# Moving VectorE's state update ahead of the output steps, and the scaled residual one slot earlier

## The chip, the cores and the metric

The kernel runs on one core of a Trainium2 chip. The metric is the device time of one launch in microseconds; less is better. The profile's engine names are PE (TensorE matmuls), PEld (TensorE weight loads), DVE (VectorE), ACT (ScalarE), POOL (GpSimd) and SP (the queue that issues the DMAs).

## The reference

The input is eight sequences of 512 tokens with 128 features. Each goes through a layer norm, a state-space attention block with its own RMS norm and residual, a second layer norm and a mixture of expert feed-forward networks with a residual. What touches this change is the scan of the attention block:

```python
def step(h, inp):
    x_c, dt_c, B_c, C_c = inp
    lcs = jnp.cumsum(dt_c * A, axis=1)
    lcsT = jnp.transpose(lcs, (0, 2, 1))
    M = jnp.exp(jnp.where(mask, lcsT[:, :, :, None] - lcsT[:, :, None, :], -jnp.inf))
    G = jnp.einsum('blhn,bihn->bhli', C_c, B_c)
    intra = jnp.einsum('bhli,bihp->blhp', M * G, x_c)
    inter = jnp.einsum('blh,blhn,bhpn->blhp', jnp.exp(lcs), C_c, h)
    total_decay = jnp.exp(lcsT[:, :, -1])
    h_new = total_decay[:, :, None, None] * h + jnp.einsum('bhl,blhp,blhn->bhpn', M[:, :, -1, :], x_c, B_c)
    return (h_new, intra + inter)
...
y = y + x_h * D[None, None, :, None]
y = y * jax.nn.silu(z)
y = rmsnorm(y, w_norm_out)
return residual + y @ w_out_proj
```

The output of a chunk (`intra + inter`) and its new state (`h_new`) both need products of the chunk, but not each other.

## The kernel before

A sequence is worked in chunks of 128 tokens, four of them (`c` = 0 to 3), for 8 heads as 4 pairs. The work of three sequences is interleaved: `body(s, prev, older)` runs 24 slots `i` (0 to 23), in which every engine does the attention of sequence `s` and the feed-forward blocks of sequence `prev` (and the last four blocks of `older`). Each engine runs a list of instructions in the order in which the code writes them; semaphores join the lists.

**Feed-forward blocks.** In slot `i` block `b = i - 4` is begun. TensorE makes three products of it into a bank of PSUM (`first`, L360 to L362, out of `fTh`/`fTl`), ScalarE writes `act_h` (L757), VectorE writes `act_l` (`act_low`, L1105), and two slots later TensorE makes three more (`second`, L562 to L564). There are two such banks, so `first(b)` waits only for the `act_l` of block `b - 2`. Every fourth block VectorE also writes a product of the expert's output and its weights (`routed_out`, L1113), before `second` may overwrite its bank, and GpSimd adds it up (L1299).

**The scan.** From slot 12 on a chunk takes three slots.

- Step 0: TensorE makes the segments of the decays (`segments`, L441) in two halves of four matmuls. The first half writes bank `MAIN[0]` and waits until VectorE has read the outputs of the last chunk there (`y_steps`). The second half writes `MAIN[1]` and waits for `state_step`, the state update of the last chunk, which reads `MAIN[1]`. Then come `b_tokens` (L451). ScalarE turns the segments into `decay` (eight instructions, L781), then copies `btok` (L785). GpSimd makes `xw` (L1286) and masks `decay` (L1290).
- Step 1: TensorE transposes the last chunk's `yz` (`y_transposes`, L498), after `btok` has been copied, since both use one bank. Then come the Gram products (L464). VectorE multiplies them by the decay into `mg` (L984).
- Step 2: TensorE makes, in this order, the products with the state (L473), the chunk's own part of the new state (L478, `s_psum`), and the products within the chunk (L485, `y_psum`). VectorE's `attend(..., 2)` follows: it waits for `y_psum`, makes `yt` (L991 for c = 0; L995, L999, L1001 after that) and `yz` (L1006); then, for c below 3, `state_m = state * tdx` (L1010) and the two halves of `state` (L1023, for c = 0 a copy, L1021). Only after these does it turn to the slot's `act_low`.

At the end of the chunk's slot TensorE is at `first` and `second`, and then at `segments` of the next chunk.

**The residual.** `residual(s)` makes two small columns (L913, L914) and four products of 128x128 (`xr`, L917). It reads only what `norm1` left; `add_residual` reads `xr` in the next body, and the DMA of the next sequence's `x_in` waits for it. VectorE's order in slots 8 to 11 is: `dt_decay` (L946 to L950), `act_low` of slots 8 and 9, `l_parts` (L955 to L963, it waits for ScalarE's `ecs_ready`), `residual`, `gT_copy` (L1100), `act_low` of slot 10, `lT_copy` (L971). TensorE waits for `l_parts` at L426 and for `gT_copy` at L537.

In sequence 0 there are no feed-forward blocks yet; in its place stands the folding of the weights (L580, L583, DVE L889, ACT L699, POOL L1226 and L1231).

Of the kernel before, what the change touches and what calls it, by code (L numbers as in the profile page):

```python
# [7 lines left out]
ALU = mybir.AluOpType  # L8
# [6 lines left out]
P = 128  # L15
NCH = 4
# [4 lines left out]
NP = NH // 2  # L21
HD = DI // NH
# [18 lines left out]
def nth(s, per, k):  # L41


    if isinstance(s, int) and s * per + k <= 0:
        return None
    return s * per + k


def is_seq(s, n):

    return isinstance(s, int) and s == n


def build(nc, a, out):
# [4 lines left out]
    with ExitStack() as ctx:  # L59
        def sb(name, shape, dt=F32):  # L60
            return ctx.enter_context(nc.sbuf_tensor(name, shape, dt))

        def sem(name):
            return ctx.enter_context(nc.semaphore(name))
# [5 lines left out]
        MAIN = bank[4:8]  # L70
# [83 lines left out]
        tdx = sb("tdx", [P, NCH, NP])  # L154
# [9 lines left out]
        state = sb("state", [P, NP, 2 * HD])  # L164
        state_m = sb("state_m", [P, NP, 2 * HD])
# [86 lines left out]
        y_psum = sem("y_psum")  # L252
        s_psum = sem("s_psum")
        state_step = sem("state_step")
# [613 lines left out]
        def _(dve):  # L868
            v_ = nc.vector
# [42 lines left out]
            def residual(s):  # L912
                v_.tensor_scalar(one_rs[:], rs1[:, 0, :], 1.0, None, ALU.add).then_inc(xr_scales, 1)  # L913
                v_.tensor_tensor(mean_rs[:], mv1[:, :, 0], rs1[:, 0, :], ALU.mult).then_inc(xr_scales, 1)  # L914
                dve.wait_ge(xr_scales, nth(s, 2, 2))
                for c in range(NCH):
                    v_.tensor_scalar(xr[:, c, :], x_in[:, c, :], one_rs[:, c:c + 1], mean_rs[:, c:c + 1], ALU.mult, ALU.subtract)\  # L917
                        .then_inc(xr_ready, 1)
# [17 lines left out]
            def dt_add(s, c):  # L936
                dve.wait_ge(sz_ready, nth(s, 4, c + 1))
                v_.tensor_tensor(dtv[:, c, :], MAIN[(c + 2) % 4][:, DI:2 * DI], b_dt[:], ALU.add).then_inc(dtv_ready, 1)

            def dt_clamp(s):  # L940
                dve.wait_ge(dtv_ready, nth(s, 4, 4))
                v_.tensor_scalar(sp[:], dtv[:], CLAMP, None, ALU.min).then_inc(dt_clamped, 1)

            def dt_decay(s):
                dve.wait_ge(dt_log, nth(s, 1, 1))
                v_.tensor_tensor(dtv[:], dtv[:], sp[:], ALU.max).then_inc(dt_steps, 1)  # L946
                dve.wait_ge(dt_steps, nth(s, 3, 1))
                v_.tensor_reduce(dsum[:], dtv[:].rearrange("p c (h d) -> p (c h) d", d=HD), AX_X, ALU.add).then_inc(dt_steps, 1)
                dve.wait_ge(dt_steps, nth(s, 3, 2))
                v_.tensor_tensor(dta[:].rearrange("p (c h) -> p c h", h=NH), dsum[:].rearrange("p (c h) -> p c h", h=NH),  # L950
                                 a_neg[:].unsqueeze(1).to_broadcast([P, NCH, NH]), ALU.mult).then_inc(dt_steps, 1)
# [13 lines left out]
            def l_parts(s):  # L965
                dve.wait_ge(ecs_ready, nth(s, 4, 4))
                three_parts(TR[:, 0:32].rearrange("p (c h) -> p c h", h=NH), lparts, rem1, rem2, lpart_steps, s, 5, 0)

            def lT_copy(s):
                dve.wait_ge(lT_psum, nth(s, 1, 1))  # L970
                v_.tensor_copy(lT[:], TR_BF[0:3 * NH, :]).then_inc(lT_ready, 1)  # L971

            def c_copy(s, b):
                dve.wait_ge(proj_psum, nth(s, 14, b + 11))
                v_.tensor_copy(CT[:, b, :], MAIN[b][:]).then_inc(c_ready, 1)

            def attend(s, c, step):
                if step == 1:
                    for hf in range(2):
                        dve.wait_ge(g_psum, nth(s, 8, 2 * c + hf + 1))  # L980
                        dve.wait_ge(decay_masked, nth(s, 8, 2 * c + hf + 1))
                        if hf == 0 and (v := nth(s, 4, c)) is not None:
                            dve.wait_ge(y_psum, v)
                        v_.tensor_tensor(mg[:, hf, :, :].rearrange("p n l -> p (n l)"), MAIN[2 + hf][:],  # L984
                                         decay[:, hf, :, :].rearrange("p n l -> p (n l)"), ALU.mult).then_inc(mg_ready, 1)
                if step == 2:

                    dve.wait_ge(y_psum, nth(s, 4, c + 1))
                    dve.wait_ge(xd_ready, nth(s, 4, c + 1))
                    if c == 0:  # L990
                        v_.tensor_tensor(yt[:], MAIN[0][:, 0:DI], xd[:], ALU.add).then_inc(y_steps, 1)  # L991
                        dve.wait_ge(y_steps, nth(s, 10, 1))
                    else:
                        first = 3 * c - 2
                        v_.tensor_tensor(yt[:].rearrange("p (h d) -> p h d", h=NH),  # L995
                                         MAIN[0][:, DI:2 * DI].rearrange("p (h d) -> p h d", h=NH),
                                         ecs[:, c, :].unsqueeze(2).to_broadcast([P, NH, HD]), ALU.mult).then_inc(y_steps, 1)
                        dve.wait_ge(y_steps, nth(s, 10, first + 1))
                        v_.tensor_tensor(yt[:], MAIN[0][:, 0:DI], yt[:], ALU.add).then_inc(y_steps, 1)  # L999
                        dve.wait_ge(y_steps, nth(s, 10, first + 2))  # L1000
                        v_.tensor_tensor(yt[:], yt[:], xd[:], ALU.add).then_inc(y_steps, 1)  # L1001
                        dve.wait_ge(y_steps, nth(s, 10, first + 3))
                    if (v := nth(s, 4, c)) is not None:
                        dve.wait_ge(ssq_ready, v)
                        dve.wait_ge(yT_psum, v)
                    v_.tensor_tensor(yz[:], yt[:], sz[:, c, :], ALU.mult).then_inc(yz_ready, 1)  # L1006
                    if c < NCH - 1:
                        first = (0, 2, 5)[c]
                        if c > 0:
                            v_.tensor_tensor(state_m[:], state[:], tdx[:, c, :].unsqueeze(2).to_broadcast([P, NP, 2 * HD]),  # L1010
                                             ALU.mult).then_inc(state_step, 1)
                            dve.wait_ge(state_step, nth(s, 8, first + 1))
                            first += 1
                        dve.wait_ge(s_psum, nth(s, 3, c + 1))
                        if (v := nth(s, 4, c + 1 if c > 0 else 0)) is not None:
                            dve.wait_ge(y_psum, v)
                        own = MAIN[1][:, 0:256].rearrange("p (n d) -> p n d", n=NP)
                        for t in range(2):
                            q, d = slice(64 * t, 64 * t + 64), slice(HD * t, HD * t + HD)
                            if c == 0:  # L1020
                                v_.tensor_copy(state[q, :, d], own[q, :, d]).then_inc(state_step, 1)  # L1021
                            else:
                                v_.tensor_tensor(state[q, :, d], own[q, :, d], state_m[q, :, d], ALU.add).then_inc(state_step, 1)  # L1023
                        dve.wait_ge(state_step, nth(s, 8, first + 2))

            def mean_square(s):
                dve.wait_ge(ssq_ready, nth(s, 4, 4))
# [97 lines left out]
            def scan_part(s, i):  # L1125
                last = is_seq(s, n_seq - 1)
                if i == 2:
                    dt_add(s, 0)
                    dt_add(s, 1)
                if i == 3:  # L1130
                    dt_add(s, 2)
                if i == 4:
                    dt_add(s, 3)
                    dt_clamp(s)
                if i == 7:
                    c_copy(s, 0)
                if i == 8:
                    dt_decay(s)
                if i == 10:
                    l_parts(s)  # L1140
                    residual(s)
                if i == 11:
                    lT_copy(s)
                if i >= CHUNKS_FROM:
                    attend(s, *divmod(i - CHUNKS_FROM, 3))
                if i == 15 and not last:
                    norm1(s + 1)
                if i == 18 and not last:
                    norm1_apply(s + 1)

            def body(s, prev, older):
                for i in range(NBLK):
# [5 lines left out]
                    if s is not None:  # L1158
                        if i == 0:
                            conv(s, 0, (0, 1))  # L1160
                        scan_part(s, i)
# [185 lines left out]
```

## Time and profile before

| | |
|---|---|
| median of 3 runs | 759.35 us (758.93 to 760.9) |
| the profiled execution | 760.49 us, its span 758.4 us |
| mean granted TensorE clock | 0.946 |
| PE busy | 656.0 us (86%) |
| PEld busy | 514.7 us (68%) |
| DVE busy | 477.1 us (63%) |
| ACT busy | 359.9 us (47%) |
| POOL busy | 176.7 us (23%) |

A time of an engine is the sum over its instructions; the rest of the span it waited. The profiled execution took 2.1 us more than its span, and 1.14 us more than the median. The granted clock is the share of full speed (2.4 GHz) that TensorE had; 0.5 is 1.2 GHz.

### The profile page before, as it was taken

How to read it: one execution, taken by the hardware profiler on the slowest of the kernel's cores; microseconds unless marked ns; L12 is line 12 of the kernel's file. 1: busy time of each engine (PE TensorE's matmuls, PEld its weight loads, DVE VectorE, ACT ScalarE, POOL GpSimd, SP SyncE). 2: the span in 40 equal slices, each digit the busy share in tenths (PEclk: the TensorE clock that was granted, in tenths of full speed). 3: DMA queues.
4: the chain of work that ended last, by engine and by line, in shares of the span. 5: the costliest groups of instructions: out<-in, count | busy, mean ns of one | idle time of the engine just before them, and what ended most of it. 6: DMA issues, size and time to landing. Idle time of an engine off the chain costs nothing.

```text
span 758.4 us, 11829 instructions
## 1 busy us (share of the span) xinstructions
PE 656.0 (86%) x3890; PEld 514.7 (68%) x3890; DVE 477.1 (63%) x1148; ACT 359.9 (47%) x837; POOL 176.7 (23%) x249
## 2 busy tenths in 40 slices
PE   4477869989889988989889988999989988988896
PEld 3355857677767766777767766777767766776664
DVE  6654266566766587467767587467767587465544
ACT  3624136634564346644655346544655346542252
POOL 7146110323013210323014110323014110232002
PEclk9879579999999999999999999999999999999799
DMA  7000000000000000000000000000000000000000
GB/s 230 8 15 2 1 0 1 15 1 1 0 29 1 1 1 1 29 1 1 0 28 0 0 0 8 20 0 0 0 28 0 0 1 15 1 1 0 15 1 14
DMA packets 12345, 8.89 MB, mean 12 GB/s; under 512 B 1259, under 2 KB 10902, under 8 KB 12310
## 3 DMA queue, kind: packets, MB, share of 16 engines
q1 hardware_dynamic: 12310, 8.44, 3.6%
q8 instruction: 20, 0.33, 0.2%
q14 instruction: 15, 0.12, 0.1%
HBM read 6.34 MB, written 2.10 MB: 11 GB/s over the span
## 4 chain that ended last, share of the span: by engine, by line
PE 49%; DVE 24%; issue 6%; ACT 5%; POOL 0%; DVEq 0%; POOLq 0%; ACTq 0%
PE bank L485 7%; PE bank L360 6%; PE bank L362 5%; PE bank L361 5%; PE bank L464 4%; PE bank L562 4%; PE bank L563 3%; PE bank L564 3%; DVE act_l L1105 3%; PE bank L478 2%; PE bank L473 2%; ACT decay L781 2%; DVE cv L933 2%; PE bank L506 1%; PE bank L441 1%
## 5 line engine op out<-in xcount | busy, mean ns | idle before, releaser
L757 ACT ACTIVATE act_h<-bank 128x512 fp32r<-128x512 f32 x192 | 116.8, 609 | 205.2 <-PE bank L362 203.2
L1105 DVE SCALAR_TENSOR_TENSOR act_l<-bank,act_h 128x512 fp32r<-128x512 f32 x192 | 131.2, 687 | 117.3 <-ACT act_h L757 115.3
L360 PE MATMUL bank<-fTl,w1h 128*128 128x512 f32 x192 | 92.2, 480 | 22.1 <-DVE fTl L1060 11.2
L1299 POOL TENSOR_TENSOR late<-late 128x512 f32<-128x512 f32 x32 | 41.4, 1293 | 259.7 <-DVE late L1113 259.7
L781 ACT ACTIVATE decay<-bank,lneg 128x128 f32<-128x128 f32 x256 | 71.2, 382 | 35.4 <-PE bank L441 35.4
L562 PE MATMUL bank<-act_l,w2h 128*128 128x512 f32 x192 | 80.1, 417 | 3.7 <-DVE act_l L1105 2.2
L563 PE MATMUL bank<-act_h,w2l 128*128 128x512 f32 x192 | 78.0, 406 | 0.0
L362 PE MATMUL bank<-fTh,w1h 128*128 128x512 f32 x192 | 77.9, 406 | 0.0
L564 PE MATMUL bank<-act_h,w2h 128*128 128x512 f32 x192 | 77.6, 404 | 0.0
L361 PE MATMUL bank<-fTh,w1l 128*128 128x512 f32 x192 | 77.3, 402 | 0.0
L360 PEld LDWEIGHTS bank<-fTl,w1h 128*128 128x128 f32 x192 | 36.8, 191 | 44.5 <-DVE act_l L1105 32.6
L485 PE MATMUL bank<-xs,mg 128*128 128x32 f32 x512 | 65.2, 283 | 0.0
L485 PEld LDWEIGHTS bank<-xs,mg 128*128 128x128 f32 x512 | 63.0, 201 | 0.7
L1286 POOL TENSOR_TENSOR xw<-xs,decay 128x128 f32<-128x128 f32 x48 | 19.5, 406 | 181.6 <-ACT decay L781 116.8
L995 DVE TENSOR_TENSOR yt<-bank,ecs 128x256 f32<-128x256 f32 x24 | 10.2, 425 | 68.5 <-PE bank L485 68.5
L984 DVE TENSOR_TENSOR mg<-bank,decay 128x512 f32<-128x512 f32 x64 | 41.1, 682 | 16.7 <-PE bank L464 16.4
L562 PEld LDWEIGHTS bank<-act_l,w2h 128*128 128x128 f32 x192 | 36.9, 192 | 18.4 <-DVE act_l L1105 6.2
L564 PEld LDWEIGHTS bank<-act_h,w2h 128*128 128x128 f32 x192 | 37.2, 194 | 9.1
L362 PEld LDWEIGHTS bank<-fTh,w1h 128*128 128x128 f32 x192 | 37.1, 193 | 8.9
L563 PEld LDWEIGHTS bank<-act_h,w2l 128*128 128x128 f32 x192 | 37.3, 194 | 7.7
L1290 POOL TENSOR_SCALAR_AFFINE_SELECT decay<-decay 128x508 f32<-128x508 f32 x64 | 41.2, 644 | 0.0
L464 PE MATMUL bank<-CT,BT 64*128 64x128 f32 x512 | 40.0, 299 | 0.0
(193 smaller groups left out, 1258.3 us busy)
## 6 DMA issues: line engine op xcount, KB each, us to landing
x_in<-L_attn_hidden_dram SPq DMA_DIRECT2D x8, 256.0 KB, 2.8
out_dram<-late SPq DMA_DIRECT2D x8, 256.0 KB, 2.8
late<-L_ffn_sw_dram SPq DMA_DIRECT2D x2, 512.0 KB, 6.3
late<-L_ffn_rw_dram SPq DMA_DIRECT2D x1, 1024.0 KB, 6.7
CT<-L_attn_w_in_proj_dram SPq DMA_DIRECT2D x1, 772.0 KB, 4.6
b_dt<-L_attn_b_dt_dram SPq DMA_DIRECT2D x1, 128.0 KB, 3.3
w_out_raw<-L_attn_w_out_proj_dram SPq DMA_DIRECT2D x1, 128.0 KB, 3.5
rows<-L_ffn_sb_dram SPq DMA_DIRECT2D x1, 4.0 KB
```

The source lines that it names most:

```text
L360: mm(dst, stat_h, mov_l, start=True, stop=False)
L361: mm(dst, stat_l, mov_h, start=False, stop=False)
L362: return mm(dst, stat_h, mov_h, start=False, stop=True)
L464: ins = mm(MAIN[2 + hf][:, at(n)], BT[q, n, at(c)], CT[q, n, at(c)], start=True, stop=True)
L485: ins = mm(MAIN[0][:, h * HD:(h + 1) * HD], mg[:, hf, n, :], xs[:, c, h * HD:(h + 1) * HD], start=True, stop=True)
L562: mm(FOUT[:], w2h[:, g, k, :], act_l[:, r, :], start=begins, stop=False)
L563: mm(FOUT[:], w2l[:, g, k, :], act_h[:, r, :], start=False, stop=False)
L564: mm(FOUT[:], w2h[:, g, k, :], act_h[:, r, :], start=False, stop=ends).then_inc(second_done, 1)
L757: nc.scalar.activation(act_h[:, b % RING, :], HID[b % 2][:], ACT.Relu).then_inc(act_h_ready, 1)
L781: ins = nc.scalar.activation(decay[:, hf, n, :], MAIN[hf][:, at(n)], ACT.Exp, bias=lneg[:, c, 2 * n + hf:2 * n + hf + 1])
L1105: v_.scalar_tensor_tensor(act_l[:, r, :], HID[b % 2][:], 0.0, f(act_h[:, r, :]), ALU.max, ALU.subtract)\
L1299: g.tensor_tensor(acc, acc, term, ALU.add).then_inc(acc_ready, 1)
```

## The change

In step 2 the whole state update (L1010, L1021 and L1023) moves ahead of the wait for `y_psum`, so it waits for `s_psum` alone, and its own wait for `y_psum` goes. `residual(s)` is called in slot 9, ahead of that slot's `act_low`, and no longer in slot 10 behind `l_parts`. No instruction is added or removed on any engine.

```diff
                 if step == 2:
 
+                    if c < NCH - 1:
+                        first = (0, 2, 5)[c]
+                        if c > 0:
+                            v_.tensor_tensor(state_m[:], state[:], tdx[:, c, :].unsqueeze(2).to_broadcast([P, NP, 2 * HD]),
+                                             ALU.mult).then_inc(state_step, 1)
+                            dve.wait_ge(state_step, nth(s, 8, first + 1))
+                            first += 1
+                        dve.wait_ge(s_psum, nth(s, 3, c + 1))
+                        own = MAIN[1][:, 0:256].rearrange("p (n d) -> p n d", n=NP)
+                        for t in range(2):
+                            q, d = slice(64 * t, 64 * t + 64), slice(HD * t, HD * t + HD)
+                            if c == 0:
+                                v_.tensor_copy(state[q, :, d], own[q, :, d]).then_inc(state_step, 1)
+                            else:
+                                v_.tensor_tensor(state[q, :, d], own[q, :, d], state_m[q, :, d], ALU.add).then_inc(state_step, 1)
+                        dve.wait_ge(state_step, nth(s, 8, first + 2))
+
                     dve.wait_ge(y_psum, nth(s, 4, c + 1))
                     dve.wait_ge(xd_ready, nth(s, 4, c + 1))
...
                     v_.tensor_tensor(yz[:], yt[:], sz[:, c, :], ALU.mult).then_inc(yz_ready, 1)
-                    if c < NCH - 1:
-                        first = (0, 2, 5)[c]
...
-                        dve.wait_ge(s_psum, nth(s, 3, c + 1))
-                        if (v := nth(s, 4, c + 1 if c > 0 else 0)) is not None:
-                            dve.wait_ge(y_psum, v)
...
-                        dve.wait_ge(state_step, nth(s, 8, first + 2))
...
                 if i == 8:
                     dt_decay(s)
+                if i == 9:
+                    residual(s)
                 if i == 10:
                     l_parts(s)
-                    residual(s)
```

## Rows read from the trace of the kernel before

**Rows 1.** Waits, whole span: us in total, times, longest us.

```profile
DVE yt L995 <- PE bank L485: 68.5, 24, 5.7
...
PE bank L441 <- DVE state L1023: 15.3, 14, 1.3
...
PE bank L537 <- DVE gT L1100: 7.8, 7, 1.1
```

**Rows 2.** VectorE's groups by line: count, busy us, mean ns, idle before.

```profile
L1023 DVE TENSOR_TENSOR state<-bank,state_m 64x128 f32<-64x128 f32 x32 | 9.2, 289 | 1.7 <-DVE state_m L1010 0.8
...
L917 DVE TENSOR_SCALAR xr<-x_in,one_rs,mean_rs 128x128 f32<-128x128 f32 x32 | 8.9, 342 | 0.3
...
L1010 DVE TENSOR_TENSOR state_m<-state,tdx 128x256 f32<-128x256 f32 x16 | 6.7, 418 | 0.0
...
L1021 DVE COPY state<-bank 64x128 f32<-64x128 f32 x16 | 4.6, 285 | 0.2
```

**Rows 3.** Timeline, sequence 3, chunk 1 to 2: start, duration, instruction, idle before.

```profile
321.05 0.69 DVE L1105 SCALAR_TENSOR_TENSOR act_l<-bank,act_h 128x512 fp32r<-128x512 f32 x1 [0.25 <-ACT act_h L757]
...
321.77 1.06 PE L478 MATMUL bank<-xw,btok 128*128 128x64 f32 x8
...
324.62 0.43 DVE L995 TENSOR_TENSOR yt<-bank,ecs 128x256 f32<-128x256 f32 x1 [2.88 <-PE bank L485]
...
326.00 0.39 PE L441 MATMUL bank<-lT,pick_head 24*128 24x128 bf16 x4
...
326.79 0.61 DVE L1023 TENSOR_TENSOR state<-bank,state_m 64x128 f32<-64x128 f32 x2
327.46 0.39 PE L441 MATMUL bank<-lT,pick_head 24*128 24x128 bf16 x4 [1.07 <-DVE state L1023]
...
328.95 1.32 POOL L1299 TENSOR_TENSOR late<-late 128x512 f32<-128x512 f32 x1 [8.23 <-DVE late L1113]
...
329.74 0.38 PE L498 MATMUL bank<-ident,yz 128*128 128x128 f32 x2
```

**Rows 4.** Timeline, sequence 3, chunk 0 to 1.

```profile
314.74 0.62 PE L441 MATMUL bank<-lT,pick_head 24*128 24x128 bf16 x8
...
317.96 0.44 PE L498 MATMUL bank<-ident,yz 128*128 128x128 f32 x2 [0.61 <-ACT btok L785]
```

**Rows 5.** Timeline, sequence 3, chunk 2 to 3.

```profile
337.72 0.39 PE L441 MATMUL bank<-lT,pick_head 24*128 24x128 bf16 x4
...
343.37 0.39 PE L562 MATMUL bank<-act_l,w2h 128*128 128x512 f32 x1
```

**Rows 6.** Timeline, sequence 5, chunk 2 to 3.

```profile
508.76 0.93 PE L441 MATMUL bank<-lT,pick_head 24*128 24x128 bf16 x8
...
513.58 0.19 PEld L562 LDWEIGHTS bank<-act_l,w2h 128*128 128x128 f32 x1 [0.52 <-DVE late L1113]
```

**Rows 7.** Timeline, sequence 0: slots 10 and 11, two ends of chunks.

```profile
34.68 6.65 POOL L1226 TENSOR_TENSOR w2l<-late,w2h 128x3072 fp32r<-128x3072 f32 x1 [15.75 <-ACT w2h L694]
34.99 0.19 DVE L955 CAST lparts<-bank 128x32 bf16<-128x32 f32 x1 [1.82 <-ACT tdx L747]
...
35.44 5.93 DVE L959 CAST lparts<-rem 128x32 bf16<-128x32 f32 x1
...
41.98 1.11 DVE L917 TENSOR_SCALAR xr<-x_in,one_rs,mean_rs 128x128 f32<-128x128 f32 x4
...
70.22 0.69 DVE L889 SCALAR_TENSOR_TENSOR late<-bank,late 128x512 f32<-128x512 f32 x1
...
86.71 0.60 PE L441 MATMUL bank<-lT,pick_head 24*128 24x128 bf16 x4 [1.29 <-DVE state L1023]
```

**Rows 8.** Timeline, sequence 3, slots 8 to 11.

```profile
298.56 1.28 DVE L1105 SCALAR_TENSOR_TENSOR act_l<-bank,act_h 128x512 fp32r<-128x512 f32 x2
...
302.69 0.60 PE L537 MATMUL bank<-gT,pick_expert 12*128 12x512 bf16 x2 [1.11 <-DVE gT L1100]
```

**Rows 9.** Windows: stretch, busy us by engine (PE, PEld, DVE, ACT, POOL), PE clock.

```profile
424.00:428.00 4.00, 4.00 (x22) 3.04 (x23) 1.67 (x3) 2.41 (x8) 2.29 (x5) 0.57 0.00 0
```

More of the change, by code:

```diff
@@ L1006, in attend @@
                     v_.tensor_tensor(yz[:], yt[:], sz[:, c, :], ALU.mult).then_inc(yz_ready, 1)
-                    if c < NCH - 1:
-                        first = (0, 2, 5)[c]
[L1009 to L1013, printed above, removed]
-                        dve.wait_ge(s_psum, nth(s, 3, c + 1))
-                        if (v := nth(s, 4, c + 1 if c > 0 else 0)) is not None:
-                            dve.wait_ge(y_psum, v)
[L1017 to L1023, printed above, removed]
-                        dve.wait_ge(state_step, nth(s, 8, first + 2))
             def mean_square(s):
```

## The prediction

> **What bounds the kernel now.** I read the waits first: who stands still, and for whom. The longest idle of VectorE inside the scan is ahead of the output's first step: 68.5 us in 24 waits for L485, the last products of step 2. TensorE, busiest of the engines, in turn stands 15.3 us in 14 waits before the second half of the segments, for L1023, the last instruction of the state update [rows 1]. So at the end of a chunk VectorE idles for TensorE, and then TensorE idles for VectorE.
>
> The timeline of one chunk's end shows the order [rows 3]. L478, which the state update needs, runs from 321.77 to 322.83. VectorE's last work, act_l, ends at 321.74. It then waits 2.88 us for L485, starts yt at 324.62, and reaches the two state halves at 326.79, ending at 327.40. TensorE made the first half of the segments at 326.00 and starts the second at 327.46. Eight L441 take 0.62 us [rows 4] and four take 0.39, so the second half starts 0.23 us behind the first when nothing holds it, and 1.2 us are lost here, of which the row gives 1.07 as idle matmul time.
>
> The 14 waits are: sequences 1 to 7, each at the end of chunks 1 and 2, less the end of chunk 1 in sequence 2 and of chunk 2 in sequence 5, where TensorE came late by itself; and both ends in sequence 0. After chunk 0 there is none: the eight L441 of 314.74 run together [rows 4].
>
> **Part 1, the state update moves.** It costs VectorE the same: 0.42 us for L1010 and two L1023 (0.61 us together, [rows 3]), or two L1021 of 0.285 us for chunk 0 [rows 2]. In its new place it begins with L1010 at 321.74, ends that at 322.16, waits for L478 (322.83) and ends at about 323.5. The output is ready at 324.58, so 1.1 us of the idle time is left, and yt starts no later. What it gives back is 1.04 us of VectorE between yz and act_l, and the wait at L441. This cover would be gone only if L485 ended over 1.1 us sooner against L478.
>
> How much of it TensorE keeps depends on what is late next, so I look for places where the second half of the segments had no wait.
>
> *End of chunk 1.* Behind the segments stand ScalarE's eight decays and the copy of btok, for which L498 waits. Where all eight L441 run together, L498 comes 317.96 - 314.74 = 3.22 us after the first, held by btok [rows 4]. At the end of chunk 1 it is 329.74 - 326.00 = 3.74 us [rows 3]. The first half will start no sooner, and ScalarE's chain hangs on it, so I take 0.5 us, not 1.2. Six sequences: 3.0 us. (Bounds: 0 if anything else binds there, 1.2 if btok didn't.)
>
> *End of chunk 2.* No btok is needed. The next joint is L562, which waits for L1113, which waits for act_l, act_h and the decays ahead of it on ScalarE. In sequence 3 L562 comes 343.37 - 337.72 = 5.65 us after the first L441 [rows 5]. In sequence 5 the eight L441 ran together, and L562 came after 513.58 - 508.76 = 4.82 us, held by L1113 [rows 6]; its L441 were slower, 0.93 us against 0.62 [rows 4, 6], so 4.6 us at full clock. I take 1.0 us. Six sequences: 6.0 us. (Bounds: 0.8 by the row as it stands, 1.2 by the whole wait.)
>
> *Sequence 0.* After chunk 1, ScalarE's decays stand behind a copy that waits for VectorE's L889, which starts at 70.22 directly behind the state update [rows 7]; it moves up by 1.0 us. After chunk 2 nothing else stands between, and the wait is 1.29 us of idle matmul time at 1.2 GHz [rows 7], some 1.5 us from start to start. Together 2.5 us.
>
> *Chunk 0*, eight times: TensorE had no wait and the copy goes into an idle stretch. 0 us.
>
> Nothing is queued behind a new wait. VectorE stands at s_psum before it stands at y_psum, and TensorE signals them in that order; no DMA hangs on either.
>
> **Part 2, the residual moves.** Its 1.4 us (four L917 of 0.34 [rows 2], and two small ones) go ahead of act_l of slot 9. That act_l ends at 299.84 [rows 8] and will end at about 301.2; its first reader is in slot 11, whose first matmul is 302.69 [rows 8], so 1.4 us of cover remain. l_parts then comes 1.3 us later, and L426 with it, but gT follows l_parts directly: the same work stands between 298.56 and gT, whose end is what TensorE waits 1.11 us for [rows 8]. Before, VectorE idled some 0.1 us for ScalarE's ecs_ready there; now the residual fills it. I take 0.1 us in seven sequences, 0.7 us. (Bounds: a gain of 0.16; a loss of 1.4 us each if something read that act_l in slot 10, which the code does not show.) The DMA of x_in is issued some 1.4 us sooner and is needed four slots later: 0.
>
> In sequence 0 the residual stood between l_parts and lT, at 41.98 [rows 7]. In slot 9 it fills VectorE's wait of 1.82 us for ScalarE ahead of L955 [rows 7], and lT comes up to TensorE's transposes, 0.4 us sooner.
>
> This is where a rule speaks against the move. In sequence 0 GpSimd's L1226 starts at 34.68 and takes 6.65 us, and the cast L959, of 32 columns, takes 5.93 us beside it [rows 7]. The Trainium skill (GPSIMD Engine Reference, Key points) says that GpSimd shares its SBUF interfaces with VectorE, and that instructions in a two-port mode or with two SBUF inputs contend; by that rule, the trace agrees. L917 and L1010 are of these kinds. By the rows L917 would run from about 33.3 to 34.5, just ahead of L1226; were it caught, l_parts would start after 41.3 instead of being held in its midst, 0.4 us worse than now. In the other sequences GpSimd is idle there, and at the new place of L1010 too: L1299 at 328.95 has 8.23 us of idle before it [rows 3]. So contention changes the sum by at most 0.8 us.
>
> **Sum.** 3.0 + 6.0 + 2.5 + 0.7 + 0.4 = 12.6 us. The profiled execution took 760.49 us, so it would take 747.9; it stood 1.14 us over the median, so against the median of 759.35 that is 746.8, and I say 747.0.
>
> **TensorE's clock.** In five places of the steady part the clock falls to 1.2 GHz for a while, as between 424 and 428 with a mean of 0.57 [rows 9]. Before this one stood the products of L485, then the gap at L441. Work in such a stretch takes at most twice as long: (1 - 0.57) x 4 = 1.7 us lost at most. Two of the five follow the gap after chunk 2, and may vanish with it (3.4 us); others may come. I leave this out of the sum and in the range.
>
> **The rivals.**
>
> *A, the sum as above, 743.5 to 750.5:* 0.62. For it speaks that both takers of the gain (btok, L1113) are seen at work in rows of this trace.
>
> *B, the whole gap comes back.* If L498 and L562 move with the segments, the ends of chunks 1 and 2 give 1.2 us twelve times, 14.4 and not 9.0, and two slow stretches vanish: 759.35 - 12.6 - 5.4 - 3.4 = 738 at most, half of it 742.5. Against it: rows 4 and 6 show the takers. 0.12.
>
> *C, most is handed back later.* Behind the scan stand waits between VectorE, ScalarE and TensorE at each sequence's turn, or slow stretches come at two or three more places. With half of part 1 left the sum is 6.3 us: 753; range 750.5 to 757. What speaks against it: these waits hang on the same chain, which moves as a whole. 0.20.
>
> *D, no change:* the wait at L441 is replaced by one of the same length in the same place. The margin of 1.1 us of idle before yt would have to be wrong. 757 to 761.6. 0.04.
>
> *E, slower,* by one mechanism: the clock. The packed order brings the stretches poor in columns (L473, L478, L485) into a steady rhythm, and the clock falls behind each. To be slower by 0.3% it must eat 12.6 + 2.3 = 14.9 us, nine more stretches at 1.7 us, on top of the five. There are 14 such places, the ends of chunks 1 and 2 in sequences 1 to 7. Nothing in the trace shows such a rhythm. 0.02.
>
> **How the numbers follow.** The likeliest is A, 747. The range takes A, and the nearer parts of B and C: 742.5 to 753. A measurement of this kernel can tell about 0.3%, 2.3 us, from no change. Faster is A, B and C: 0.94. Same is D: 0.04. Slower is E: 0.02.
>
> **What the profile after would show.** The row of waits PE L441 for L1023 gone or near 0; VectorE's wait for L485 shorter by 1.0 us each where c is 1 or 2, and by some 0.6 for chunk 0; L1010 starting right behind act_l; the eight L441 together at every end of a chunk; L498 held by btok, 3.2 us behind the first L441, also after chunk 1; L562 held by L1113 after chunk 2; a period of the steady part of about 1.5 us less, near 1.6 with the residual. For part 2: L917 directly ahead of act_l in slot 9, L426 1.3 us later, L537 in its old place. Wrong would be: a new wait of TensorE for act_l in slots 9 to 11, yt starting later than before against L485, or a count of slow stretches far from five.

## The result

The changed kernel takes 736.62 us (734.72 to 737.6, 4 runs) against 759.67 us of the kernel before beside it: a ratio of 0.9692, 95% interval 0.9668 to 0.9716. It is 23 us faster. The prediction said 12.6 us, and 736.6 lies below its range. Two of the executions told of below, one of the kernel before (860.47 us at clock 0.702) and one with the state update alone (751.23 us at 0.945), count as slow and are left out of the means and ratios.

| | before | after |
|---|---|---|
| profiled execution, its span | 760.49, 758.4 us | 737.6, 735.9 us |
| granted TensorE clock | 0.946 | 0.967 |
| time at 1.2 GHz, 2 x (1 - clock) x span | 81.9 us | 48.6 us |
| PE busy | 656.0 us | 645.3 us |
| VectorE busy | 477.1 us | 474.8 us |

First the waits of the changed kernel over the whole span, to be held against [rows 1] (us in total, times, longest). The state's lines are now L991, L1000 and L1002, yt is L1008 to L1018, and L485 and L441 are as before.

```profile
DVE yt L1012 <- issue: 20.1, 16, 2.7
DVE yt L1012 <- PE bank L485: 18.4, 8, 2.7
...
PE bank L426 <- DVE lparts L963: 14.6, 8, 8.0
DVE state L1002 <- PE bank L478: 14.5, 16, 2.1
...
PE bank L498 <- ACT btok L785: 11.0, 16, 2.8
...
PEld bank L441 <- DVE yt L1016: 5.6, 13, 1.2
```

TensorE's wait at L441 for the state update is gone. VectorE's idle ahead of yt was 68.5 us; it is now split: 38.5 us there (the profile puts the 16 of chunks 1 and 2 down to no releaser) and 14.5 us ahead of the state. TensorE's new waits are those for btok and for L426.

Now the timeline of the changed kernel, sequence 4, from the end of chunk 1 to the start of chunk 3 (start, duration, instruction, idle before).

```profile
395.83 0.41 DVE L991 TENSOR_TENSOR state_m<-state,tdx 128x256 f32<-128x256 f32 x1
395.94 1.06 PE L478 MATMUL bank<-xw,btok 128*128 128x64 f32 x8
...
397.10 0.61 DVE L1002 TENSOR_TENSOR state<-bank,state_m 64x128 f32<-64x128 f32 x2 [0.85 <-PE bank L478]
...
398.85 0.43 DVE L1012 TENSOR_TENSOR yt<-bank,ecs 128x256 f32<-128x256 f32 x1 [1.14 <-issue]
...
400.17 0.62 PE L441 MATMUL bank<-lT,pick_head 24*128 24x128 bf16 x8
...
403.38 0.44 PE L498 MATMUL bank<-ident,yz 128*128 128x128 f32 x2 [0.45 <-ACT btok L785]
...
411.42 0.61 PE L441 MATMUL bank<-lT,pick_head 24*128 24x128 bf16 x8
...
415.23 0.74 DVE L1112 SCALAR_TENSOR_TENSOR late<-bank,cols,late 128x512 f32<-128x512 f32 x1
...
416.02 0.50 PE L562 MATMUL bank<-act_l,w2h 128*128 128x512 f32 x1 [0.18 <-DVE late L1112]
```

The update ends at 397.71, and 1.14 us of idle are left before yt. The eight L441 run together both times. L498 follows the first of them by 403.38 - 400.17 = 3.21 us, held by btok (3.74 before, [rows 3]); L562 follows the first L441 of the next chunk by 416.02 - 411.42 = 4.60 us, held by L1112 (5.65 before, [rows 5]).

The period of a sequence is read from L948, which runs once in each. First two pairs of the kernel before, sequences 1 and 3, neither with a stretch at 1.2 GHz:

```profile
128.80 1.22 DVE L948 TENSOR_REDUCE dsum<-dtv 128x32 f32<-128x1024 f32 x1
...
212.43 1.22 DVE L948 TENSOR_REDUCE dsum<-dtv 128x32 f32<-128x1024 f32 x1
...
297.20 1.22 DVE L948 TENSOR_REDUCE dsum<-dtv 128x32 f32<-128x1024 f32 x1
...
381.35 1.22 DVE L948 TENSOR_REDUCE dsum<-dtv 128x32 f32<-128x1024 f32 x1
```

and of the changed kernel, sequences 1 and 4, again at full clock:

```profile
123.20 1.22 DVE L948 TENSOR_REDUCE dsum<-dtv 128x32 f32<-128x1024 f32 x1
...
205.30 1.22 DVE L948 TENSOR_REDUCE dsum<-dtv 128x32 f32<-128x1024 f32 x1
...
371.61 1.22 DVE L948 TENSOR_REDUCE dsum<-dtv 128x32 f32<-128x1024 f32 x1
...
454.15 1.22 DVE L948 TENSOR_REDUCE dsum<-dtv 128x32 f32<-128x1024 f32 x1
```

Sequence 1 went from 83.6 to 82.1 us; a sequence of the loop from 84.2 (sequence 3) to 82.5 (sequence 4). That is 1.5 to 1.6 us each, as forecast. The eight sequences at that rate make 12 to 13 us, and not 23; so the surprise lies elsewhere. Between L948 of sequence 0 and that of sequence 1 the time fell from 97.1 to 90.5 us (31.7 to 128.8; 32.7 to 123.2), from that of sequence 7 to the end from 121.3 to 115.7 us: 6.6 and 5.6 us, where the steps of the prediction give about 3.0 and 1.6. The six periods between fell by 11.3 us together (508.3 to 497.0), where they give about 8.1. The start-up went the other way: L948 of sequence 0 comes 1.0 us later.

In these two parts the clock differs most. Windows of the kernel before (stretch, busy us of PE, PEld, DVE, ACT, POOL, granted clock, DMA):

```profile
72.50:103.50 31.00, 24.56 (x122) 22.04 (x123) 8.93 (x19) 8.96 (x27) 6.22 (x12) 0.50 0.00 1
697.00:714.50 17.50, 15.60 (x50) 11.90 (x50) 7.22 (x18) 3.58 (x7) 1.28 (x1) 0.61 0.00 1
```

and of the changed kernel at the same work:

```profile
72.00:90.00 18.00, 15.69 (x91) 14.23 (x91) 5.18 (x11) 5.42 (x19) 4.81 (x11) 0.53 0.00 1
92.00:100.00 8.00, 5.84 (x23) 5.15 (x24) 3.45 (x8) 3.24 (x6) 1.01 (x1) 0.57 0.00 0
...
678.00:696.00 18.00, 14.18 (x66) 10.45 (x67) 11.16 (x31) 5.29 (x10) 1.72 (x2) 1.00 0.04 11
```

In sequence 0 the clock was at 1.2 GHz for 31 us without a break; now it is so for some 17 and 7. (Both kernels have another stretch of 17 and 14 us there, from 31.6 and 34.5 us on.) Sequence 7's end had 14 us of it before, and has none now. In the six periods between, four stretches (13.6 us, from 239.8, 424.2, 506.1 and 594.8 on) became two (6.8 us, from 314.4 and 563.6 on).

### The profile page after: what moved, and what is told of

Read it like the earlier page. It is cut to its first block, busy times and chain, and to the rows that moved or that the text cites. A ratio compares the mean times of both kernels' runs of the same rounds, so it can differ in the third digit from the quotient of the medians.

```text
span 735.9 us, 11806 instructions
## 1 busy us (share of the span) xinstructions
PE 645.3 (88%) x3890; PEld 504.3 (69%) x3890; DVE 474.8 (65%) x1148; ACT 357.4 (49%) x837; POOL 175.2 (24%) x249
## 4 chain that ended last, share of the span: by engine, by line
PE 37%; DVE 22%; issue 15%; ACT 6%; POOL 5%; DVEq 0%; POOLq 0%; ACTq 0%
PE bank L485 5%; PE bank L360 5%; DVE act_l L1104 4%; PE bank L362 4%; PE bank L361 4%; PE bank L562 3%; ACT decay L781 3%; PE bank L563 3%; PE bank L564 3%; DVE cv L933 2%; PE bank L464 2%; POOL decay L1290 2%; PE bank L506 2%; PE bank L478 2%; PE bank L473 1%
## 5 line engine op out<-in xcount | busy, mean ns | idle before, releaser
L360 PE MATMUL bank<-fTl,w1h 128*128 128x512 f32 x192 | 91.1, 475 | 22.1 <-DVE fTl L1059 11.2
L781 ACT ACTIVATE decay<-bank,lneg 128x128 f32<-128x128 f32 x256 | 69.6, 387 | 30.5 <-PE bank L441 30.5
L562 PE MATMUL bank<-act_l,w2h 128*128 128x512 f32 x192 | 79.7, 415 | 5.3 <-DVE late L1112 2.7
L362 PE MATMUL bank<-fTh,w1h 128*128 128x512 f32 x192 | 76.3, 397 | 0.0
L564 PE MATMUL bank<-act_h,w2h 128*128 128x512 f32 x192 | 76.1, 396 | 0.0
L485 PE MATMUL bank<-xs,mg 128*128 128x32 f32 x512 | 63.6, 279 | 0.0
L485 PEld LDWEIGHTS bank<-xs,mg 128*128 128x128 f32 x512 | 61.4, 196 | 0.6
L562 PEld LDWEIGHTS bank<-act_l,w2h 128*128 128x128 f32 x192 | 36.3, 189 | 23.0 <-DVE late L1112 9.0
L360 PE MATMUL bank<-hTl,wh 128*128 128x512 f32 x80 | 34.4, 430 | 4.8 <-DVE hTl L922 3.6
```

The lines of the kernel that those rows point to most:

```text
L360: mm(dst, stat_h, mov_l, start=True, stop=False)
L362: return mm(dst, stat_h, mov_h, start=False, stop=True)
L485: ins = mm(MAIN[0][:, h * HD:(h + 1) * HD], mg[:, hf, n, :], xs[:, c, h * HD:(h + 1) * HD], start=True, stop=True)
L562: mm(FOUT[:], w2h[:, g, k, :], act_l[:, r, :], start=begins, stop=False)
L564: mm(FOUT[:], w2h[:, g, k, :], act_h[:, r, :], start=False, stop=ends).then_inc(second_done, 1)
L781: ins = nc.scalar.activation(decay[:, hf, n, :], MAIN[hf][:, at(n)], ACT.Exp, bias=lneg[:, c, 2 * n + hf:2 * n + hf + 1])
```

## The experiments

Every execution reports its span and clock, so its time at 1.2 GHz is known. Over 88 executions of the 14 kernels below, taken as deviations from the mean of their own kernel, the time moves by 0.325 us for each us at 1.2 GHz (correlation 0.92; single kernels give 0.24 to 0.47, except the changed one, whose four executions all stood at 0.967 and give no slope). "Base" is a kernel's mean time less 0.325 times its mean time at 1.2 GHz: an estimate of what is left when the clock's share is taken away, not a time that was measured.

| kernel | ratio (95%) | mean us | us at 1.2 GHz | base |
|---|---|---|---|---|
| before | 1 | 760.1 | 78.6 | 734.5 |
| after | 0.969 (0.967 to 0.972) | 736.4 | 48.5 | 720.6 |
| state update only | 0.976 (0.970 to 0.982) | 741.2 | 56.2 | 722.9 |
| residual only | 0.997 (0.994 to 1.000) | 758.2 | 78.1 | 732.8 |
| before, short lag | 1.002 (1.000 to 1.004) | 761.8 | 78.3 | 736.3 |
| before, lag | 1.009 (1.006 to 1.011) | 764.3 | 80.5 | 738.1 |
| before, long lag | 1.007 (1.004 to 1.010) | 765.3 | 79.8 | 739.4 |
| after, short lag | 0.973 (0.969 to 0.977) | 741.3 | 54.4 | 723.7 |
| after, lag | 0.977 (0.974 to 0.980) | 742.3 | 53.0 | 725.0 |
| before, gap filled | 0.993 (0.988 to 0.997) | 753.5 | 57.9 | 734.7 |
| after, sequence 0 filled | 0.970 (0.966 to 0.973) | 736.1 | 41.1 | 722.7 |
| the same, L1226 late | 0.965 (0.961 to 0.968) | 732.4 | 35.5 | 720.9 |
| after, btok early | 0.960 (0.956 to 0.965) | 729.1 | 60.0 | 709.5 |
| all three | 0.950 (0.944 to 0.956) | 721.2 | 38.2 | 708.8 |

A ratio is taken against the executions of the kernel before made beside that kernel. The theories at the start: (1) the removed waits are worth the 12 or 13 us forecast, and the rest is time at 1.2 GHz that went with them; (2) the move is worth all of it directly, at places I had not counted.

### The two parts alone

State update only:

```diff
-                if i == 9:
-                    residual(s)
                 if i == 10:
                     l_parts(s)
+                    residual(s)
```

> The state update is moved, the residual stays in slot 10. Theory 1 (12 to 13 us are the removed wait, of them 11.5 by this part, and some 10 us come from less time at 1.2 GHz): 736 to 745 us, and in each period without a stretch at 1.2 GHz 1.5 us less than before (83.6 and 84.2 us before for sequences 1 and 3). Theory 2 (the state update's move is worth the whole 23 us directly): 737.5 us, the time of the changed kernel plus 1, whatever the clock does. The eight L441 run together at each chunk's end by either.

Residual only: the kernel before, with the opposite edit.

> The residual is moved to slot 9, the state update stays behind the output's steps. Both theories: 1.1 us less than before directly (0.1 us a sequence, 0.4 us in sequence 0), L426 1.3 us later, L537 in its place. Theory 1 adds what the clock does, up to 5 us either way, with time at 1.2 GHz other than the 83 us of before; theory 2 says 758.5 us.

The state update alone gave 740.61 us (median of three; 742.75 with the fourth, 751.23), the residual alone 757.51. Of the 14 us in the base the first has 11.6 and the second 1.7; the state update alone also took 22 us of time at 1.2 GHz away (16 with the fourth execution), the residual next to none. The kernel with the state update alone shows the clock's price: 738.13 us at clock 0.967, 740.61 at 0.963, 744.88 at 0.956. At one and the same program that is 6.8 us for 0.011 of clock. Theory 2, for which the clock counts nothing, falls with this. The residual alone is not told from no change: its ratio is 0.994 to 1.000, so the 1.1 us forecast for it is neither confirmed nor refuted.

### Is it the place where the clock happens to fall?

My first form of theory 1 was that the stretches fall where the program happens to stand. So I shifted both kernels by a pure delay in the start-up:

```diff
             norm1_apply(0)
+            v_.memset(state_m[:], 0.0).then_inc(lag_done, 1)
+            for k in range(4):
+                dve.wait_ge(lag_done, k + 1)
+                v_.tensor_tensor(state_m[:], state_m[:], state_m[:], ALU.add).then_inc(lag_done, 1)
             dve.wait_ge(w_scaled, 1)
```

with 4 (lag), 2 (short lag) and 6 (long lag) instructions.

> The kernel before, with five small instructions ahead of VectorE's weight splits, some 2 us of pure delay in the start-up, nothing else. Theory 1: the place of each stretch at 1.2 GHz depends on where the program stands at a given time, so the delay changes which stretches occur; the time differs from before by 2 us and by a few us more of the clock's, either way, and time at 1.2 GHz differs from 83 us by 5 or more. Theory 2: plus 2 us, no more, with the same stretches.

> The changed kernel with the same delay of some 2 us. Theory 1: between 737 and 745 us, with time at 1.2 GHz other than 51 us; periods without such a stretch stay at 82.1 and 82.5 us. Theory 2: 738.5 us, and 22 to 23 us less than the delayed kernel before.

> The kernel before with two instead of four of the delaying instructions, about 1 us. If the clock's part is a matter of where the program stands when it falls: some 761 us, and time minus 0.34 us for each us at 1.2 GHz is 734 us within 1.5, while the time at 1.2 GHz is anywhere from 70 to 90 us. If the kernel before has more time at 1.2 GHz than the changed one whatever the place: over 68 us here too.

> The changed kernel with the same short delay. By the fit: base 721 us within 1.5; if the changed kernel has less time at 1.2 GHz whatever the place, 40 to 60 us of it and 735 to 741 us; if the 30 us less were luck of the place, up to 80 us of it and up to 748 us.

> The kernel before with six of the delaying instructions, about 3 us. Base by the fit 736 to 738 us. If its time at 1.2 GHz hangs on the place alone, it may fall to 50 us here and the time to 754 us; if the kernel before has more of it whatever the place, 68 us or more and 760 to 767 us.

The medians are 765.31 us for the kernel before with the lag, 762.1 with the short and 765.7 with the long one; for the changed kernel 741.98 with the lag and 741.27 with the short one. Single stretches did move. But the mean moved little: the kernel before has 78.6, 78.3, 80.5 and 79.8 us at 1.2 GHz under four delays, the changed one 48.5, 54.4 and 53.0 under three. The three bases forecast by the fit were all too low: 736.3 us and not 734 within 1.5, 723.7 and not 721 within 1.5, 739.4 and not 736 to 738. The base rose by 2 to 5 us, more than the 1 to 3 us that I took the delay for; in the profiled executions L948 of sequence 0 came 1.7, 2.1 and 5.2 us later (kernel before), 2.0 and 3.6 (changed), so the delay itself was larger. So chance of place doesn't explain the 30 us less, and that form of theory 1 is wrong: at each delay tried the changed kernel has 24 to 30 us less at 1.2 GHz. One part does come and go: at sequence 7's end the changed kernel has none in its profiled execution, and 14 us in that with the short lag.

### Does the idle gap bring the clock down?

The kernel before, its wait for the state update untouched, but TensorE working in it; the extra products are used by nothing:

```diff
+                    if c > 1 and hf == 1:
+                        for k in range(4):
+                            mm(MAIN[2 + k % 2][:], wh[:, X0:X0 + P], hTh[:], start=True, stop=True)
                     if c > 0 and hf == 1:
                         pe.wait_ge(state_step, nth(s, 8, (2, 5, 8)[c - 1]))
```

> The kernel before, with four extra matmuls of 512 columns (0.93 us, into banks free at that time) between the two halves of the segments at the end of chunks 1 and 2, where TensorE stands idle; their products are used by nothing. The wait for the state update stays. Theory 1a (the clock falls because of this idle gap): the four or five stretches at 1.2 GHz in the steady part go, time 753 to 757 us. Theory 1b (the stretches follow the products poor in columns and the chance of where they fall, the gap has no part): 3 to 6 such stretches, time 759 to 763 us. Theory 2 (the clock counts for nothing): 760.5 us.

The median is 754.36 us. The base is that of before (734.7 and 734.5), as it should be where only idle time is filled, and the time at 1.2 GHz fell from 78.6 to 57.9 us. 20.7 x 0.325 = 6.7 us, and the mean fell by 6.6 (by 5.6 against the executions beside it; the ratio is 0.988 to 0.997). So the same work gets faster when TensorE is given more to do and its clock rises. The time lies where theory 1a put it. But the stretches did not go: the profiled execution has three in the six steady periods, as theory 1b allows, and 5.9 of its 6.8 us are won in sequence 0, which took 91.1 us and not 97.1 with 17 us less at 1.2 GHz. Its windows:

```profile
60.00:80.00 20.00, 16.38 (x136) 13.71 (x136) 8.14 (x19) 6.53 (x21) 10.12 (x13) 1.00 0.01 1
80.00:100.00 20.00, 15.34 (x83) 12.59 (x84) 8.89 (x23) 6.76 (x18) 3.14 (x6) 0.66 0.00 1
```

and those of the kernel before:

```profile
60.00:80.00 20.00, 15.93 (x115) 13.50 (x116) 7.60 (x17) 6.11 (x19) 9.70 (x13) 0.81 0.00 1
80.00:100.00 20.00, 15.23 (x77) 13.56 (x77) 6.34 (x15) 4.04 (x14) 3.15 (x6) 0.50 0.00 1
```

In the first 20 us the clock is now 1.00 and not 0.81. TensorE was busy for 16.38 - 15.93 = 0.45 us more; that is less than the added work, since the rest ran faster.

Is this what the changed kernel does too? In sequence 0, no. Here is TensorE at the start of the last chunk but one, in the kernel before, in the changed one and with the gap filled (lines shifted there: L440 are the added products, L501 is L498):

```profile
70.25 0.39 PE L441 MATMUL bank<-lT,pick_head 24*128 24x128 bf16 x4 [0.72 <-DVE state L1023]
...
74.17 0.69 PE L498 MATMUL bank<-ident,yz 128*128 128x128 f32 x2 [2.95 <-ACT btok L785]
...
69.23 0.62 PE L441 MATMUL bank<-lT,pick_head 24*128 24x128 bf16 x8
...
73.28 0.69 PE L498 MATMUL bank<-ident,yz 128*128 128x128 f32 x2 [2.85 <-ACT btok L785]
...
69.89 1.19 PE L440 MATMUL bank<-hTh,wh 128*128 128x512 f32 x4
...
74.59 0.44 PE L501 MATMUL bank<-ident,yz 128*128 128x128 f32 x2 [2.60 <-ACT btok L788]
```

The changed kernel has no gap at L441, and its clock falls all the same, in the wait for btok: L498 takes 0.69 us, as before. Only the added products keep it up through that wait (0.44 us). What the changed kernel has there is an earlier rise, at 89 us and not at 103.

In the steady part, half. The 4 us before a fall of the clock, at 239.8 and 424.2 us in the kernel before, at 314.4 in the changed one, at 319.1 with the gap filled:

```profile
235.80:239.80 4.00, 4.00 (x36) 3.91 (x35) 0.91 (x2) 0.43 (x1) 0.11 (x1) 1.00 0.00 0
420.20:424.20 4.00, 2.77 (x19) 1.90 (x19) 3.27 (x8) 2.04 (x7) 0.62 (x2) 0.99 0.00 0
...
310.40:314.40 4.00, 4.00 (x34) 3.83 (x34) 2.24 (x6) 0.60 (x1) 0.54 (x1) 1.00 0.00 0
...
315.10:319.10 4.00, 4.00 (x36) 3.88 (x34) 1.07 (x2) 0.60 (x1) 0.28 (x1) 1.00 0.00 0
```

In the kernel before two of the four falls stand behind a gap of 1.23 us at L441 (424.2 and 594.8), the other two (239.8 and 506.1) behind 4.00 us of unbroken work on TensorE that ends in L473, L478 and L485. In the changed kernel and with the gap filled no fall stands behind such a gap; all of them there, two and three, come behind unbroken work. So both ways of closing the gap are without the falls behind it, 6.8 us at 1.2 GHz in one execution of each. The gap was not the only thing that brought the clock down.

### Can the clock be kept up in sequence 0?

```diff
+                    if is_seq(s, 0):
+                        if i == 18:
+                            pe.wait_ge(fold_set, NG)
+                        for k in range({18: 9, 19: 3, 20: 4, 21: 6, 22: 3}.get(i, 0)):
+                            mm(HID[k % 2][:], wh[:, X0:X0 + P], hTh[:], start=True, stop=True)
```

> The changed kernel, with 25 extra matmuls of 512 columns in slots 18 to 22 of sequence 0, where TensorE waits and has no feed-forward blocks; their products are used by nothing. If time at 1.2 GHz in sequence 0 costs 0.4 us for each us, as it does between runs of the kernel with the state update moved alone: 24 of its 37 us go, and the time is 727 to 730 us. Rival (chains of ScalarE and VectorE bind there, the clock costs nothing): 735 to 738 us.

A miss: 736.03 us, which lies in the range of the rival. The clock did rise; between 60 and 104 us of the profiled execution it is 0.96, against 0.73 in the changed kernel:

```profile
60.00:104.00 44.00, 36.60 (x255) 30.03 (x256) 23.48 (x61) 15.31 (x44) 14.94 (x21) 0.96 0.00 1
```

The part from sequence 0's L948 to sequence 1's took 88.0 us and not 90.5, with 14 us less at 1.2 GHz; but over the four executions the time at 1.2 GHz fell by 7.4 us only, not by 24, and the base rose by 2.1 us. That the extra products also stand where TensorE had work is likely, and not shown. That a us at 1.2 GHz costs less in sequence 0, as the rival has it, doesn't follow: filling the gap won 5.9 us there for 17 us at 1.2 GHz, 0.35 us each.

### The cast beside GpSimd

```diff
             def body(s, prev, older):
-                if is_seq(s, 0):
-                    w2_low()
...
+                if is_seq(s, 0):
+                    w2_low()
                 if s is not None:
                     rsqrt_y(s)
```

> As the run before, and GpSimd's L1226 (6.65 us) issued at the end of sequence 0 instead of ahead of chunk 0, where VectorE's cast L959 stood 5.93 us beside it. If contention with it was the cause: L959 takes 0.2 to 0.9 us, and the time is 5 us below that of the kernel with filling alone, 722 to 725 us. Rival (L1226 binds in its new place too, since the first sum of sequence 1 waits for it, or holds VectorE's instructions there): less than 2 us below.

The result is 732.87 us, 3 us below the run before it: less than the 5 forecast, more than the rival's 2, and hardly clear of noise (the ratios are 0.961 to 0.968 and 0.966 to 0.973). The timeline of this kernel (lines shifted: the cast is L964, GpSimd's sum L1231, yt L1023):

```profile
36.01 0.18 DVE L964 CAST lparts<-rem 128x32 bf16<-128x32 f32 x1
...
77.83 6.67 POOL L1231 TENSOR_TENSOR w2l<-late,w2h 128x3072 fp32r<-128x3072 f32 x1
...
82.24 2.55 DVE L1023 TENSOR_TENSOR yt<-yt,xd 128x256 f32<-128x256 f32 x1
```

The cast takes 0.18 us where it took 5.93 [rows 7], so GpSimd's instruction was the cause. But beside it in its new place yt, a sum of two operands in SBUF, takes 2.55 us instead of 0.42, as the rival said for its second case. What this costs was not measured. Sequence 0 got 4.6 us shorter all the same (83.4 us from L948 to L948, 88.0 in the run before); the profiled execution lost 4.1 us again behind L948 of sequence 7, with 10 us at 1.2 GHz there.

### The taker at the end of a chunk

```diff
                     ins.then_inc(decay_ready, 1)
-                if c < NCH - 1:
-                    act.wait_ge(btok_psum, nth(s, 3, c + 1))
-                    nc.scalar.copy(btok[:], TR[:]).then_inc(btok_ready, 1)
+                    if hf == 0 and c < NCH - 1:
+                        act.wait_ge(btok_psum, nth(s, 3, c + 1))
+                        nc.scalar.copy(btok[:], TR[:]).then_inc(btok_ready, 1)
```

> The changed kernel, with ScalarE's copy of btok between the two halves of the decays instead of behind them. If btok is what takes back a part of the gain at the end of chunk 1: TensorE's wait at L498 (11.0 us in 16) goes to under 3, and 3 to 6 us are won, 731 to 734 us. Rival (the second half of the decays comes 0.48 us later, GpSimd's mask and mg with it, and these bind instead): no gain, 735 to 738 us.

729.48 us, better than expected. The waits of this kernel show the taker gone (16 waits, 17.5 us by the weight loads and 11.0 by the products, in the changed kernel):

```profile
PEld bank L498 <- ACT btok L785: 2.3, 2, 2.1
```

The base fell by 11 us, twice what I expected: a sequence of the loop at full clock takes 81.0 us instead of 82.5. That is nearly the whole of the 11.0 us that the products waited for btok (1.8 us are left); what I had taken off for the decays behind it was not lost. The clock gave some of it back, with 60.0 us at 1.2 GHz against 48.5.

### All three together

> The changed kernel with all three: sequence 0 filled with the 25 extra matmuls, L1226 at the end of sequence 0, btok copied between the halves of the decays. The time of an execution follows base + 0.34 us for each us at 1.2 GHz in the executions so far. If the three gains in the base add up (11.3 us of btok, some 0 of the filling, 2 of L1226 by those fits), and the clock is at 1.2 GHz for 40 to 55 us: 720 to 725 us. Rival (the mask behind btok and the clock take it back): no better than 729 us.

720.52 us, in the range, 5% below the kernel before (0.950, 0.944 to 0.956), and the best of all. The base, 708.8, is hardly below that of btok alone, so the 2 us of L1226 did not add; what the other two add is clock, 38.2 us at 1.2 GHz and not 60.0.

## Why the prediction was wrong

**The end of chunk 1** was forecast at 3.22 us from L441 to L498 and measured 3.21. **The end of chunk 2**: 4.6 forecast, 4.60 measured. **The cover before yt**: 1.1 and 1.14 us. **The period**: 1.5 to 1.6 us less, measured 1.5 and 1.6. Reading the taker at a place of the same trace where the wait was absent was right both times.

**The residual**: from act_l of slot 8 to L537 it was 302.69 - 298.56 = 4.13 us [rows 8], and is 376.90 - 372.97 = 3.93:

```profile
372.97 0.68 DVE L1104 SCALAR_TENSOR_TENSOR act_l<-bank,act_h 128x512 fp32r<-128x512 f32 x1
...
373.83 1.11 DVE L917 TENSOR_SCALAR xr<-x_in,one_rs,mean_rs 128x128 f32<-128x128 f32 x4
...
374.86 0.68 DVE L1104 SCALAR_TENSOR_TENSOR act_l<-bank,act_h 128x512 fp32r<-128x512 f32 x1
...
376.58 0.39 PE L426 MATMUL bank<-ident_bf,lparts 128*24 128x128 bf16 x4 [0.91 <-DVE lparts L963]
...
376.90 0.60 PE L537 MATMUL bank<-gT,pick_expert 12*128 12x512 bf16 x2
```

0.2 us at this place, where I took 0.1. In sequence 0 the cast was still held from within l_parts, as forecast, and lT came as soon as TensorE's transposes let it.

**The sum** of the direct terms, 12.6 us, stands against 13.9 us in the base.

**The step that failed** is the one on the clock: "I leave this out of the sum and in the range." I gave it 3.4 us on the side of gain, from two stretches that follow the gap. It was worth about 30 x 0.325 = 9.8 us, an estimate from the slope between executions. The parts of the profiled executions say the same without it: sequence 0, the six periods and the end give 3.6, 3.2 and 4.0 us more than the steps of the prediction, less the 1.0 us of the start-up. Those two stretches did vanish, as I had said they may. The mistake is that I looked for stretches in the steady part, where there were five short ones, and passed over the long ones, 17 and 31 us in sequence 0 and 14 at the end, which make up most of the 82 us; that is where most of the time at 1.2 GHz went away. So the term was mis-sized, and set to nothing in the sum. My sign of being wrong, a count of stretches far from five, is half met: of the five in the steady part there are two left. With 9.8 us in the sum the forecast would have been 737.

**Rival B** named the low value for the wrong reason: L498 and L562 came 0.5 and 1.05 us sooner behind the first segment, as in the sum, and not by the whole 1.2. **Rival C** has a slip: with half of the 11.5 us of part 1 left the sum is 6.9 us and not 6.3; it changes nothing. **Rival E**, that the packed order would bring the clock down more often, has the wrong sign.

**What stays open.** Why the changed kernel has 30 us less at 1.2 GHz is shown for some 7 us of them at most, the stretches behind the gap in the steady part. In sequence 0 the clock falls at the same place as before and rises sooner; what decides that was not tested. Filling the gap has 21 us less, but its added products are work that the changed kernel doesn't have, and no run put the same products where there is no gap, so it may be the work and not the gap that counts. Sequence 7's end had 14 us at 1.2 GHz in the kernel before and none in the profiled execution of the changed one, but 14 us again with btok copied early and with the short lag; I can't say what decides there. The base rests on one slope for all parts of the kernel, while single kernels give 0.24 to 0.47, so the split into 13.9 and 9.8 us is good to a few us only.

## What to carry to other kernels

Work that needs only an early product should stand ahead of the wait for the late one, if the engine idles there; and what such a move is worth is read at a place of the same trace where the wait happens to be absent, by what is late next. Then give TensorE's clock a term of its own: add up (1 - clock) over the whole span before the sum is made, the start and the end of the program too, and look at what TensorE did before each fall. Here 30 of 82 us at 1.2 GHz went with a change that was not made for them; which ones would go could not be read from the trace beforehand, so the term needs a wide range. Where an engine's copy frees one that waits (btok), put it as early in its list as its input allows.

## What the runs showed of the hardware

One program's time followed its granted clock closely from one execution to the next: 738.13 us at 0.967, 740.61 at 0.963, 744.88 at 0.956.

Four more matmuls in an idle gap of TensorE at 16 places, with products that nobody used, made a kernel faster by 0.3 to 1.2%; its mean was 6.6 us lower, with 20.7 us less at 1.2 GHz.

The granted clock fell from 2.4 to 1.2 GHz behind quite different stretches: at 424.2 us of the kernel before behind 4 us with 2.77 us of matmuls and one gap of 1.23 us, at 239.8 behind 4.00 us of matmuls without a gap. With one short stretch at 1.2 GHz in it a period of the kernel with the gap filled took 85.3 to 85.5 us, without one 83.6 to 84.1.

A VectorE instruction can be held for nearly the whole of a GpSimd instruction: a cast of 32 columns took 5.93 us beside one of 6.65 us, and 0.18 us when that was moved away; a sum of two SBUF operands took 2.55 us beside it, and 0.42 us elsewhere. The Trainium skill (GPSIMD Engine Reference, Key points) names VectorE's instructions with two SBUF inputs, and those in a 2-port mode, as contending with GpSimd. The sum is of the first kind, and by that rule, the trace agrees; in which mode the cast ran no run here shows.
